# A convolution and sparse-coding kernel: one image buffer instead of two, sums from a ring of 8-row pieces, larger rings, and new orders on every engine

## The chip, the cores and the metric

The kernel runs on one core of a Trainium2 chip. Times are device microseconds of one launch, which works through all 16 images. The core's engines are TensorE (PE), VectorE (DVE), ScalarE (ACT), GpSimd (POOL) and SyncE (SP); each works through its own list of instructions in order, and they wait for each other by semaphores.

## The reference

The input is 16 images of 64 channels, 128 x 128 pixels, in float32. Two layers follow each other, both of the form "x plus something of the group-normalised x":

```
def _gn(v, G=32, eps=1e-5):      # mean and variance over 2 channels x 128 x 128
    g = v.reshape(B_, G, C_ // G, H_, W_)
    return ((g - mean) / sqrt(var + eps)).reshape(v.shape)

x = x + conv3x3_circular(_gn(x), L0_conv_weight)          # 64 -> 64 channels
x = x + patchwise_omp(_gn(x), L1_conv_dictionary)
```

The second layer cuts the image into 4 x 4 patches (1024 per image, each a vector of 64 * 16 = 1024 numbers), and rebuilds each from 5 columns ("atoms") of a dictionary of 512:

```
D = dictionary / (norm(dictionary, axis=0) + 1e-10)
h_bar = D.T @ X                       # correlations
h = h_bar
for k in 1..5:
    index = argmax(|h| where not yet chosen)
    grow a Cholesky factor L by the row of G = D.T @ D + 1e-5 I at the chosen atoms
    x_stack = solve(L L.T, h_bar[chosen]);  h = h_bar - x_stack @ G[chosen]
X_hat = D @ coeffs
```

## The kernel before, in words

An image is held with row pairs: 128 partitions (parity of the row and channel), 64 row pairs, 128 columns. Its work is split over three periods, so that in period `i` the kernel convolves image `i`, does most of the pursuit of image `i-1`, and ends and rebuilds image `i-2`. A period has these parts.

- **Statistics (`st`, ScalarE).** The first normalisation of image `i+1` is a sweep for the sum and one for the squares over each of eight 8-row pieces (L346). The second normalisation sweeps the convolution's result (`junk_sums`). A small product on TensorE (`average`) joins channels, `root` (`rt`) on ScalarE and `gn_part` (`gn`) on VectorE make the factors `fac`, and for the first normalisation the scaled weights `wc`, `wq` and, by the product `bias`, the `shift`.
- **Convolution.** Eight rounds of 12 + 24 matmuls (L1003, L1010, L1012) into one buffer, `conv_ps`. ScalarE moves each round to `xa` (`ev`, L556); only then can the next round start. SyncE loads `xh`, the rows of a round, two rounds ahead.
- **Correlation.** ScalarE makes `z` (L538) for each of 8 tiles of 128 patches, TensorE multiplies it by the atoms (`correlate`, L947), ScalarE moves the result to `h` (`h`, L549).
- **Pursuit.** The tiles are two groups of four. A *unit* is one of the 5 steps of one group of one image. `UNITS` lists the ten units of a period as (how many images back, group, step). In a unit VectorE first finishes the step before it (small algebra, then `project`: L852, L860), then takes four maxima (L743) of scores that ScalarE makes (L605), then finds the indices. GpSimd gathers numbers of the Gram matrix (L466) and its rows (L478) at the chosen atoms.
- **Rebuilding.** `coefficients` (`co`) solves for the five numbers, the plan entry `ce` (VectorE, L648, L638, L654) spreads them over 512 columns for a pair of tiles, TensorE turns each tile (`turn`, L906), ScalarE copies it to `ct` (L517), TensorE multiplies by the atoms (`recon`, L935), ScalarE moves the result to `rb` (`re`, L526), and GpSimd adds a quarter of an image in DRAM (L486).

**What sets the order.** VectorE's and ScalarE's frame is the ten units. A table says what else is done where: place `4 n + s` is unit `n`, and for ScalarE `s` is the score after which it stands (0 to 3). For VectorE `s` is 0 at the unit's start, 1 and 1.5 inside `project`, 2 after the maxima, 2.5 after the aim, 3 after the index search, 3.5 at the end. The tables are `VECTOR_PLAN`, `SCALAR_PLAN`, `ADD_PLAN` (after which unit GpSimd adds), and four of the same kind for the tail, which is what is left when the last convolution is over. TensorE's order is written out in `period` and `tail`. Three PSUM banks are shared by `corr` and `re` in the order of `BANKS`; each waits until ScalarE has moved the one before it in its bank. `room` looks this up.

Buffers around the change: `xa`, two whole images; `ce`, two tiles; `ct`, one group; `rb`, one quarter.

## Time and profile before

| | us |
|---|---|
| time, median of 3 (lowest, highest) | 3507.67 (3506.91, 3508.01) |
| span of the profiled execution | 3506.6 |
| TensorE busy | 3022.3 (86%) |
| VectorE busy | 2678.0 (76%) |
| ScalarE busy | 1724.7 (49%) |
| GpSimd busy | 1858.1 (53%) |

For the profiled execution only its span is given, from the first to the last instruction; it is 1.1 us under the median of the runs. Periods can be told apart by the copy to `shift` (L701), of which there is one per image, shortly before its first convolution. A page's row "busy, mean ns | idle before, releaser" gives the idle time of the engine before such instructions and who ended it. PEclk is the granted clock of TensorE as a share of its full 2.4 GHz.

### The profile page before, as it was taken

Reading aid. Unit: us, or ns where it says so; the run is one execution under the profiler, and the core shown is the slowest. Engines: PE = TensorE matmul, PEld = TensorE weight load, DVE = VectorE, ACT = ScalarE, POOL = GpSimd, SP = SyncE. Lnnn points to the kernel's source line nnn. Section 1 sums busy time; section 2 is a strip of 40 time slices with the busy share of each in tenths; the row PEclk is TensorE's granted clock in tenths of the full one; section 3 lists DMA queues with packets and bytes.
Section 4 is the critical chain, followed back from the end, with each engine's and each line's share of the span. In section 5 each row is a group of like instructions: output and inputs, shape, how many; then the busy total and the mean of one; then the engine's idle time right before and its main releaser. Section 6 shows DMA issues by size and latency. Waiting matters only on the chain.

```text
span 3506.6 us, 33737 instructions
## 1 busy us (share of the span) xinstructions
PE 3022.3 (86%) x9424; PEld 1289.8 (37%) x9424; DVE 2678.0 (76%) x6981; ACT 1724.7 (49%) x2899; POOL 1858.1 (53%) x1869
## 2 busy tenths in 40 slices
PE   4996889899898989989898998989898998985547
PEld 1442333344333333433333333433333443332213
DVE  1137987878788887878789787878878787987982
ACT  3554554645555464655546364554635455443212
POOL 0025555546655564565556555555555565556761
PEclk9998999999999999999999999999999999997778
DMA  3433453435345443534444354445444453441232
GB/s 115 158 130 100 154 136 121 146 94 180 73 156 136 146 134 82 193 75 160 116 146 143 97 168 99 147 104 166 124 127 140 99 159 92 130 108 48 67 66 48
DMA packets 130507, 428.31 MB, mean 122 GB/s; under 512 B 55696, under 2 KB 55952, under 8 KB 105616
## 3 DMA queue, kind: packets, MB, share of 16 engines
q0 software_dynamic: 91776, 204.20, 24.0%
q1 hardware_dynamic: 38544, 221.96, 17.4%
q8 instruction: 76, 1.25, 0.1%
q14 instruction: 111, 0.91, 0.1%
HBM read 289.70 MB, written 136.31 MB: 121 GB/s over the span
## 4 chain that ended last, share of the span: by engine, by line
PE 70%; DVE 15%; issue 7%; POOL 4%; ACT 3%; DMA 1%; ACTq 0%; POOLq 0%; DVEq 0%
PE gen_ps L935 23%; PE gen_ps L947 22%; PE conv_ps L1003 14%; PE conv_ps L1010 7%; POOL v L466 4%; DVE ce L654 3%; DVE u L852 3%; DVE top L743 2%; DVE idx L752 2%; PE ct_ps L906 2%; DVE hot L638 1%; ACT score L605 1%; DVE h L860 1%; PE gen_ps L964 1%; ACT xa L556 1%
## 5 line engine op out<-in xcount | busy, mean ns | idle before, releaser
L466 POOL DMA_INDIRECT v<-gram_rows,cell x1280 | 1262.2, 986 | 1039.3 <-DVE cell L761 669.2
L935 PE MATMUL gen_ps<-ct,dt 128*128 128x512 f32 x2048 | 945.5, 619 | 31.4 <-ACT rb L526 18.5
L947 PE MATMUL gen_ps<-dn,z 128*128 128x512 f32 x2048 | 906.2, 598 | 32.5 <-ACT z L538 31.2
L1003 PE MATMUL conv_ps<-xh,wc 128*128 128x512 f32 x1536 | 707.6, 610 | 48.1 <-ACT xa L556 47.1
L743 DVE MAX8 top<-score 128x8 f32<-128x512 f32 x640 | 420.9, 691 | 424.6 <-ACT score L605 408.6
L478 POOL DMA_INDIRECT u<-marked_rows,chosen x504 | 519.6, 1031 | 187.3 <-issue 153.2
L935 PEld LDWEIGHTS gen_ps<-ct,dt 128*128 128x128 f32 x2048 | 400.1, 199 | 534.5 <-issue 512.9
L947 PEld LDWEIGHTS gen_ps<-dn,z 128*128 128x128 f32 x2048 | 387.7, 192 | 526.2 <-issue 491.6
L605 ACT ACTIVATE score<-h 128x512 f32<-128x512 f32 x640 | 381.8, 604 | 373.6 <-DVE h L860 203.1
L852 DVE SCALAR_TENSOR_TENSOR u<-u,nl 128x512 f32<-128x512 f32 x748 | 512.7, 747 | 12.8 <-DMA u<-marked_rows,chosen 9.3
L526 ACT ACTIVATE rb<-gen_ps 128x512 f32<-128x512 f32 x256 | 277.3, 1101 | 419.6 <-PE gen_ps L935 293.4
L1003 PEld LDWEIGHTS conv_ps<-xh,wc 128*128 128x128 f32 x1536 | 294.2, 195 | 421.1 <-issue 420.0
L752 DVE FIND_INDEX8 idx<-h 128x8 uint32<-128x520 f32 x640 | 432.1, 694 | 0.0
L906 PE MATMUL ct_ps<-ident,ce 128*128 128x128 f32 x512 | 103.9, 338 | 317.1 <-DVE ce L654 272.7
L1012 PE MATMUL conv_ps<-xh,wq 64*64 64x512 f32 x1536 | 359.3, 597 | 0.0
L1010 PE MATMUL conv_ps<-xh,wq 64*64 64x512 f32 x1536 | 359.2, 597 | 0.0
L654 DVE SCALAR_TENSOR_TENSOR ce<-hot,xc,ce 128x512 f32<-128x512 f16 x512 | 359.0, 740 | 0.0
L860 DVE SCALAR_TENSOR_TENSOR h<-u,na,h 128x512 f32<-128x512 f32 x504 | 352.8, 746 | 6.9 <-DMA u<-marked_rows,chosen 5.8
L556 ACT ACTIVATE xa<-conv_ps,shift 128x1024 f32<-128x1024 f32 x128 | 142.5, 1113 | 431.7 <-PE conv_ps L1012 431.7
L538 ACT ACTIVATE z<-xa,fac 128x512 f32<-128x512 f32 x256 | 293.8, 1259 | 97.3 <-PE gen_ps L947 94.2
L906 PEld LDWEIGHTS ct_ps<-ident,ce 128*128 128x128 f32 x512 | 68.9, 168 | 388.1 <-DVE ce L654 291.3
L517 ACT ACTIVATE ct<-ct_ps 128x512 f32<-128x512 f32 x128 | 75.7, 591 | 273.0 <-PE ct_ps L906 220.6
(103 smaller groups left out, 1859.5 us busy)
## 6 DMA issues: line engine op xcount, KB each, us to landing
xh<-x_paired SPq DMA_DIRECT2D x128, 650.0 KB, 4.1
xa<-x_pairs SPq DMA_DIRECT2D x64, 1024.0 KB, 7.2
y_rows<-xa SPq DMA_DIRECT2D x64, 1024.0 KB, 9.3
y_rows<-rb POOLq DMA_DIRECT2D x64, 1024.0 KB, 8.0
v<-gram_rows,cell POOLq DMA_INDIRECT x1280
u<-marked_rows,chosen POOLq DMA_INDIRECT x504, 3.9
dn<-atoms SPq DMA_DIRECT2D x1, 2048.0 KB, 11.5
gram_rows<-u POOLq DMA_DIRECT2D x4, 256.0 KB, 2.4
```

Source lines behind the costliest of these rows:

```text
L466: pool.indirect_dma_start(v[:, g, k - 1, j, t:t + 1], None, cells, bass.IndirectOffsetOnAxis(ap=cell[:, g, k // (KMAX - 1), j, t:t + 1], a ...
L478: pool.indirect_dma_start(kept(img, g, k, t), None, marked, bass.IndirectOffsetOnAxis(ap=chosen[:, g, t:t + 1], axis=0))\
L605: act.activation(score[t % 2][:], h[:, g * T + t, 0:ATOMS], ACT.Abs).then_inc(score_ready[g], 1)
L654: dve.scalar_tensor_tensor(ce[:, place, :], hot[:, m % HOT_RING, :], coef, ce[:, place, :], ALU.mult, ALU.add).then_inc(ce_step, 1)
L743: dve.max(top8[:, t, :], score[t % 2][:]).then_inc(top_found[g], 1)
L752: dve.max_index(idx8[:, t, :], h[:, g * T + t, ATOMS:HW], h[:, g * T + t, :]).then_inc(located[g], 1)
L852: dve.scalar_tensor_tensor(kept(img, g, k, t), kept(img, g, j, t), nl[:, g, k - 1, j, t:t + 1], kept(img, g, k, t), ALU.mult, ALU.add).the ...
L860: dve.scalar_tensor_tensor(hh, kept(img, g, k, t), na[:, g, k, t:t + 1], hh, ALU.mult, ALU.add)\
L935: last = pe.matmul(to[:], dt_[:, a, d, :], ct[:, a, :], start=(a == 0), stop=(a == NA - 1))
L947: last = pe.matmul(to[:], z[:, t % 2, d // PATCH, d % PATCH, :], dn[:, d, :], start=(d == 0), stop=(d == ND - 1))
L1003: pe.matmul(conv_ps[:, a], wc[:, tap, a * CIN:a * CIN + P], rows[:, a + 1:a + 2 * CP:2, tap:tap + W], start=(tap == 0), stop=False)
L1010: pe.matmul(conv_ps[above, a], wq[second, tap, :], rows[second, a:a + 2 * CP - 1:2, tap:tap + W], start=False, stop=(tap == TAPS - 1))
```

## The change

`xa` holds one image instead of two. The image that is only summed for its statistics, the next one, comes in eight pieces of 8 row pairs through a ring `xs` of two, each loaded as soon as the piece two before is summed. So the evictions of the convolution, which write `xa`, wait for the store of the image before and for the `z` that reads it. `ce` has four places instead of two, `ct` two groups instead of one, `rb` two quarters instead of one. All order tables, TensorE's order, the banks and the tail's list of units are new. The lines of the convolution, the correlation, the turns, the reconstruction and the pursuit are as they were.

```diff
+CHUNKS = PAIRS // SWEEP
-CE_RING = 2
+CE_RING = 4
+XS_RING = 2
+RB_RING = 2
+CT_RING = 2
+CHUNK_PLAN = {
+    0: [0, 1, 2], 5: [3, 4], 7: [5, 6, 7],
+}
-TAIL = (... (2, 1, 4), (1, 1, 0), (1, 0, 2), (1, 1, 1), ...
+TAIL = (... (2, 1, 4), (1, 0, 2), (1, 1, 0), (1, 1, 1), ...
 VECTOR_PLAN = {
-    1.5: [("co", 0)], 5: [("ce", 0, 0)], 11: [("ce", 0, 1)], 24: [("co", 1), ("ce", 1, 0)],
-    30: [("ce", 1, 1), ("gn", 1, 1)], 35.5: [("gn", 0, 1)], 38: [("gn", 0, 2)],
+    0: [("co", 0)], 1.5: [("ce", 0, 0)], 9: [("ce", 0, 1)], 23: [("co", 1)], 24: [("ce", 1, 0)], 30: [("ce", 1, 1)],
+    31: [("gn", 1, 1)], 38.5: [("gn", 0, 1), ("gn", 0, 2)],
 }
-ADD_PLAN: 4: [(0, 0)], 6: [(0, 1)], 7: [(1, 0)], 9: [(1, 1)]
+ADD_PLAN: 4: [(0, 0)], 7: [(0, 1)], 9: [(1, 0), (1, 1)]
-        xa = [sb(f"xa{n}", [P, PAIRS, W]) for n in range(2)]
+        xa = sb("xa", [P, PAIRS, W])
+        xs = sb("xs", [P, XS_RING, SWEEP, W])
-        rb = sb("rb", [P, HR, W])
+        rb = sb("rb", [P, RB_RING, HR, W])
-        ct = sb("ct", [P, NA, T * P])
+        ct = sb("ct", [P, CT_RING, NA, T * P])
+        def chunk_in(eng, c, image):
+            eng.dma_start(xs[:, c % XS_RING], x[image][:, c * SWEEP:(c + 1) * SWEEP, :]).then_inc(xs_loaded[c % XS_RING], 16)
 # statistics, first normalisation, images after the first
+                    if not square:
+                        act.wait_ge(xs_loaded[c % XS_RING],
+                                    at(i - 1, 16 * CHUNKS // XS_RING, 16 * (c // XS_RING + 1)))
+                    rows = xs[:, c % XS_RING]
 # SyncE, after round r of the convolution (the loads of whole quarters go)
+                    for c in CHUNK_PLAN.get(r, ()):
+                        if here[-1]:
+                            sp.wait_ge(x_sums[0], at(i + (c >= XS_RING), SUMS[0], 2 * ((c - XS_RING) % CHUNKS) + 3))
+                            chunk_in(sp, c, i + 1)
 # ScalarE, ct
-                    if not (img == 0 and g == 0):
-                        act.wait_ge(recon_done, at(img, GROUPS * ND, g * ND))
+                    if not (img == 0 and g < CT_RING):
+                        act.wait_ge(recon_done, at(img, GROUPS * ND, (g + 1 - CT_RING) * ND))
 # ScalarE, ev
+                    if i > 0 and c % (ROUNDS // GROUPS) == 0:
+                        for ph in range(PHASES):
+                            act.wait_ge(x1_out[c // (ROUNDS // GROUPS) * PHASES + ph], at(i, 16, 0))
+                    if i > 0:
+                        act.wait_ge(z_ready, at(i - 1, TILES, c + 1))
...
```

The order changes, where a period starts on TensorE (here the one of the seventh image). `conv_ps` rows open a round of the convolution, `gen_ps<-dn,z` a correlation, `ct_ps` a turn. Before:

```order
L1003 MATMUL conv_ps<-xh,wc 128x512 [waits rows_loaded0,x1_ready,shift_ready,weights_ready]
...
L1003 MATMUL conv_ps<-xh,wc 128x512 [waits x1_ready,rows_loaded1]
...
L906 MATMUL ct_ps<-ident,ce 128x128 [waits ct_ready,ce_step]
...
L1003 MATMUL conv_ps<-xh,wc 128x512 [waits x1_ready,rows_loaded0]
...
L906 MATMUL ct_ps<-ident,ce 128x128 [waits ct_ready,ce_step]
...
L1003 MATMUL conv_ps<-xh,wc 128x512 [waits x1_ready,rows_loaded1]
...
L947 MATMUL gen_ps0<-dn,z 128x512 [waits recon_out,z_ready]
```

Now:

```order
L1023 MATMUL conv_ps<-xh,wc 128x512 [waits rows_loaded0,x1_ready,shift_ready,weights_ready]
...
L967 MATMUL gen_ps0<-dn,z 128x512 [waits recon_out,z_ready]
...
L1023 MATMUL conv_ps<-xh,wc 128x512 [waits x1_ready,rows_loaded1]
...
L926 MATMUL ct_ps<-ident,ce 128x128 [waits ct_ready,ce_step]
...
L1023 MATMUL conv_ps<-xh,wc 128x512 [waits x1_ready,rows_loaded0]
...
L967 MATMUL gen_ps1<-dn,z 128x512 [waits recon_out,z_ready]
...
L1023 MATMUL conv_ps<-xh,wc 128x512 [waits x1_ready,rows_loaded1]
```

The correlations went from behind round 3 to between the rounds, and the second turn behind round 3.

On VectorE at the start of a period, the rows from the last step of `co` on. Before:

```order
L835 TENSOR_TENSOR xc<-xc,tmp 128x4 [waits solve_step]
L743 MAX top8<-score0 128x8 [waits score_ready1,signed0]
L743 MAX top8<-score1 128x8 [waits score_ready1]
...
L747 TENSOR_TENSOR h<-top8,plus_minus 128x4x8 [waits top_found1]
L752 MAX_INDEX idx8<-h 128x8 [waits aimed1] x4
L755 TENSOR_TENSOR which<-idx8 128x4 [waits located1]
L757 TENSOR_TENSOR chosen<-idx8 128x4
```

Now:

```order
L855 TENSOR_TENSOR xc<-xc,tmp 128x4 [waits solve_step]
L668 TENSOR_SCALAR ce<-count,which,xc 128x512 [waits ce_turned,solve_step]
L668 TENSOR_SCALAR ce<-count,which,xc 128x512 [waits ce_turned]
L658 TENSOR_SCALAR hot<-count,which 128x512 [waits ce_step] x2
L674 SCALAR_TENSOR_TENSOR ce<-hot,xc,ce 128x512 [waits ce_step,hot_step] x2
...
L763 MAX top8<-score0 128x8 [waits score_ready1,signed0]
L763 MAX top8<-score1 128x8 [waits score_ready1]
```

The first `ce` pair stood one unit later and now stands ahead of the period's first maxima.

On ScalarE between the scores of the ninth and the tenth unit, down to the root of the first normalisation (`gsc0`). Before:

```order
L605 ACTIVATE score0<-h 128x512 [waits top_found0,h_updated0]
L605 ACTIVATE score1<-h 128x512 [waits top_found0,h_updated0]
L549 ACTIVATE h<-gen_ps2 128x512 [waits located0,corr_done]
L579 ACTIVATE gsc0<-conv_ps 128x3 [waits gn_sum0]
...
L526 ACTIVATE rb<-gen_ps0 128x512 [waits recon_done]
L526 ACTIVATE rb<-gen_ps1 128x512 [waits recon_done]
L538 ACTIVATE z<-xa1,fac1 128x128x4 [waits corr_done,gn_step1]
L538 ACTIVATE z<-xa1,fac1 128x128x4
L605 ACTIVATE score0<-h 128x512 [waits h_updated1]
```

Now:

```order
L625 ACTIVATE score1<-h 128x512 [waits top_found0,h_updated0]
L350 ACTIVATE xs,sums0<-xs 128x1024 [waits x_sums0,xs_loaded1]
L350 ACTIVATE xs,sums0<-xs,minus_shift0 128x1024 [waits x_sums0]
...
L553 ACTIVATE z<-xa,fac1 128x128x4 [waits corr_done,gn_step1]
...
L564 ACTIVATE h<-gen_ps1 128x512 [waits located0,corr_done]
L564 ACTIVATE h<-gen_ps0 128x512 [waits located0,corr_done]
L625 ACTIVATE score0<-h 128x512 [waits h_updated1]
L625 ACTIVATE score1<-h 128x512 [waits h_updated1]
L599 ACTIVATE gsc0<-conv_ps 128x3 [waits gn_sum0]
```

The last three pieces of the sums and two `h` now stand ahead of the tenth unit's scores, and the root behind the second of these scores.

## Rows read from the trace of the kernel before

**Rows 1.** The page, busy us, share of the span, instructions, for each engine:

```profile
PE 3022.3 (86%) x9424; PEld 1289.8 (37%) x9424; DVE 2678.0 (76%) x6981; ACT 1724.7 (49%) x2899; POOL 1858.1 (53%) x1869
```

**Rows 2.** Windows: one steady period, then three stretches inside it:

```profile
core 0: us, PE busy (x) PEld busy (x) DVE busy (x) ACT busy (x) POOL busy (x), PEclk, DMA share, GB/s
1157.60:1360.00 202.40, 184.79 (x584) 78.71 (x583) 166.00 (x434) 106.91 (x180) 113.66 (x117) 0.96 0.44 131
1241.40:1299.10 57.70, 47.35 (x154) 20.60 (x153) 47.69 (x123) 29.46 (x57) 34.66 (x37) 0.94 0.44 134
1167.00:1175.00 8.00, 7.94 (x36) 3.02 (x36) 8.00 (x16) 1.20 (x2) 4.40 (x4) 1.00 0.97 220
1179.00:1189.00 10.00, 10.00 (x41) 3.82 (x39) 9.80 (x20) 1.80 (x3) 0.00 (x0) 0.83 0.12 48
```

**Rows 3.** TensorE's waits in that period: us in total, times, longest:

```profile
PE ct_ps L906 <- DVE ce L654: 13.2, 2, 9.6
PE conv_ps L1003 <- ACT xa L556: 2.2, 2, 1.4
```

**Rows 4.** VectorE's longest waits in that period:

```profile
DVE top L743 <- ACT score L605: 26.7, 10, 8.4
```

**Rows 5.** TensorE in order of time: start, duration, operation, idle before:

```profile
1157.58 5.33 PE L1003 MATMUL conv_ps<-xh,wc 128*128 128x512 f32 x12
...
1178.76 0.66 PE L906 MATMUL ct_ps<-ident,ce 128*128 128x128 f32 x4 [3.55 <-DVE ce L654]
1179.25 7.02 PE L1003 MATMUL conv_ps<-xh,wc 128*128 128x512 f32 x12
...
1236.25 7.03 PE L947 MATMUL gen_ps<-dn,z 128*128 128x512 f32 x16
1243.12 3.60 PE L935 MATMUL gen_ps<-ct,dt 128*128 128x512 f32 x8
1246.55 5.33 PE L1003 MATMUL conv_ps<-xh,wc 128*128 128x512 f32 x12
...
1254.55 10.57 PE L935 MATMUL gen_ps<-ct,dt 128*128 128x512 f32 x24
```

**Rows 6.** VectorE in order of time, maxima of the first unit and first `ce` pair:

```profile
1158.96 2.73 DVE L743 MAX8 top<-score 128x8 f32<-128x512 f32 x4 [3.75 <-ACT score L605]
...
1170.88 1.01 DVE L648 TENSOR_SCALAR ce<-count,which,xc 128x512 f32<-128x512 f16 x2
...
1177.96 1.40 DVE L654 SCALAR_TENSOR_TENSOR ce<-hot,xc,ce 128x512 f32<-128x512 f16 x2
```

**Rows 7.** ScalarE's groups in that period: busy us, mean ns, idle before:

```profile
L538 ACT ACTIVATE z<-xa,fac 128x512 f32<-128x512 f32 x16 | 18.4, 1260 | 5.9 <-PE gen_ps L947 5.9
...
L346 ACT ACTIVATE xa<-xa,minus_shift 128x1024 f32<-128x1024 f32 x8 | 9.2, 1147 | 0.2
```

**Rows 8.** VectorE in order of time: copies to `shift` of images 1, 2, 3, 15:

```profile
171.88 0.16 DVE L701 COPY shift<-conv_ps 128x1 f32<-128x1 f32 x1 [10.42 <-PE conv_ps L989]
...
337.13 0.14 DVE L701 COPY shift<-conv_ps 128x1 f32<-128x1 f32 x1
...
540.80 0.14 DVE L701 COPY shift<-conv_ps 128x1 f32<-128x1 f32 x1
...
2968.07 0.14 DVE L701 COPY shift<-conv_ps 128x1 f32<-128x1 f32 x1
```

**Rows 9.** The page's DMA issues: KB each, median us from issue to landing:

```profile
xh<-x_paired SPq DMA_DIRECT2D x128, 650.0 KB, 4.1
xa<-x_pairs SPq DMA_DIRECT2D x64, 1024.0 KB, 7.2
```

**Rows 10.** Waits behind the last period (3181.4 to 3507), then order of time:

```profile
DVE ce L648 <- PE ct_ps L906: 9.4, 2, 5.0
...
ACT rb L526 <- DMA y_rows<-rb: 42.2, 5, 17.0
...
3452.87 0.63 PE L906 MATMUL ct_ps<-ident,ce 128*128 128x128 f32 x4 [0.84 <-ACT ct L517]
...
3460.07 1.41 DVE L654 SCALAR_TENSOR_TENSOR ce<-hot,xc,ce 128x512 f32<-128x512 f16 x2
```

More of the change, by code:

```diff
@@ L162, in lag @@
         return 0 if n < T else 1
[L163 removed]
+    return 2 if kind in ("co", "ce", "ct", "re") else 0
 def units(i, images):
@@ L455, in _ @@
                 sp.wait_ge(x1_out[n], 16 * images)
-            sp.wait_ge(recon_added, 16 * GROUPS * PHASES * images)
+            for n in range(RB_RING):
+                sp.wait_ge(recon_added[n], 16 * GROUPS * PHASES * images // RB_RING)
         @block.gpsimd
@@ L472, in gather @@
                     if img == images - 1 and g == 1 and k == 2:
-                        for n in range(GROUPS * PHASES):
-                            pool.wait_ge(x1_out[n], at(img, 16, 0))
-                        pool.wait_ge(z_ready, at(img, TILES, 0))
+                        pool.wait_ge(x_sums[0], at(img, SUMS[0], SUMS[0]))
+                    elif img == images - 1 and g == 1 and k == 3:
+                        pool.wait_ge(conv_done, at(img, ROUNDS, ROUNDS))
                     for t in range(T):
@@ L536, in extra @@
                         first = (t // T * PHASES + ph) * HR + t % T * CP
-                        rows = xa[q][:, first:first + CP, :]
+                        rows = xa[:, first:first + CP, :]
                         last = act.activation(z[:, t % 2, ph].rearrange("p j (h w) -> p h w j", h=TP // 2),
@@ L934, in recon @@
                 for a in range(NA):
-                    last = pe.matmul(to[:], dt_[:, a, d, :], ct[:, a, :], start=(a == 0), stop=(a == NA - 1))
+                    last = pe.matmul(to[:], dt_[:, a, d, :], ct[:, g % CT_RING, a, :], start=(a == 0), stop=(a == NA - 1))
                 last.then_inc(recon_done, 1)
@@ L1021, in convolve, with period @@
                     turn_atoms(c)
-            def period(i, par):
+            def period(i):
                 here = parts(i)
@@ L1027, in period @@
                     convolve(i, 0)
+                if b:
+                    correlate(i, 1, 4)
+                if own:
                     convolve(i, 1)
@@ L1043, in period @@
                     correlate(i, 1, 6)
+                if own:
+                    convolve(i, 5)
+                if b:
+                    correlate(i, 1, 7)
                 if p:
@@ L1062, in period @@
                 if p:
-                    turn(i - 2, 1, 0)
                     recon(i, 2, 0, 4)
@@ L1066, in period @@
                     recon(i, 2, 0, 6)
+                    turn(i - 2, 1, 1)
                     recon(i, 2, 0, 7)
@@ L1070, in period @@
                 if p:
-                    turn(i - 2, 1, 1)
                     turn(i - 2, 1, 2)
@@ L1085, in period @@
                     correlate(i, 0, 1)
+                if here[-1]:
+                    average(i + 1, 0)
+                if own:
                     correlate(i, 0, 2)
                 if here[-1]:
-                    bias(i + 1, 1 - par)
+                    bias(i + 1, (i + 1) % 2)
                 if p:
@@ L1107, in tail @@
                 recon(i, 2, 0, 2)
+                turn(i - 2, 1, 0)
+                turn(i - 2, 1, 1)
                 recon(i, 2, 0, 3)
@@ L1119, in tail @@
                 recon(i, 2, 1, 2)
+                turn(i - 1, 0, 0)
                 recon(i, 2, 1, 3)
@@ L1152, in _ @@
             for i in range(images):
-                period(i, i % 2)
+                period(i)
             tail(images)
```

146 lines of the change are left out of this document (71 added, 75 removed), and 70 rows, old and new, of tables (BANKS, SCALAR_PLAN, TAIL_BANKS, TAIL_SCALAR_PLAN).

## The prediction, made before the changed kernel ran

> **What bounds the kernel now.** I read the page first: TensorE is busy 86% of the span, VectorE 76%, ScalarE 49% [rows 1]. A share over the span hides where it waits, so next came one steady period in a windows query: of 202.40 us TensorE is busy 184.79, VectorE 166.00, ScalarE 106.91 [rows 2]. So TensorE stands still for 17.6 us in a period, and the list of waits says for what: 13.2 us at L906, for a `ce` that VectorE has not built (two times, the longest 9.6), and 2.2 us for the eviction L556 of the convolution buffer [rows 3]. VectorE has 36.4 us free per period, yet 26.7 us of it is spent waiting for a score that ScalarE gives late [rows 4]. The two engines wait for each other at different places of the period: no resource is full, the order is what costs.
>
> The waits cost twice. After the 3.55 us stop, the 12 matmuls of L1003 take 7.02 us, where the same 12 take 5.33 undisturbed [rows 5]; the granted clock of that stretch is 0.83 (part of it at 1.2 GHz instead of 2.4), after a stop of 1.4 us it stays at 1.00 [rows 2]. After the 9.6 us stop it is slow again; by the same ratio of 1.3 I put the two together at 4 to 5 us per period. TensorE's floor for a period is then 184.8 - 4.8 = 180. It is also the sum of its parts from undisturbed starts: a convolution 8.00, a correlation 6.87, a reconstruction 3.43 [rows 5], 8 x 8.0 + 8 x 6.95 + 16 x 3.47 + 8 turns of 0.47 + 0.5 = 179.5.
>
> **The new period, by hand.** Time 0 is the start of convolution 0. I lay the new orders along three engines with the durations of today; no instruction that computes is removed or added in a steady period but for one tiny sum.
>
> *VectorE, start.* Today the four maxima of the first unit wait 3.75 us and end at 1161.7, which is 4.1 after convolution 0 (1157.58) [rows 5, 6]; the first `ce` pair stands a unit later and takes 8.4 us (1170.88 to 1179.36 [rows 6]). The change puts the pair before these maxima, where the wait was. They need the last correlation of the period before, so they still end near 4.1 and the 8.4 us go out of what follows. The turn that waited 3.55 us finds its `ce` ready.
> *TensorE, start.* Convolution 0 ends at 8.0; correlation 4 now stands between it and convolution 1 and covers the eviction (the 1.4 us wait goes): 15, 23. Convolution 2 waits 0.8 for its eviction: 32. Correlation 5: 39. Convolution 3 needs eviction 2, which stands behind the scores of the third unit, ready near 39.3, so it starts at 41 (a new wait of 1.5) and ends at 49; convolution 4 ends at 58, correlation 6 at 65, convolution 5 at 73, correlation 7 at 80.
> *Meeting point 1.* The sixth unit's last score needs correlation 7. VectorE is there early: from the first maxima to the sixth unit's it takes 79.7 us today, of which 8.4 are the moved pair and about 3 are waits, so 68.3; it arrives at 73 and is let go at about 82.
> *VectorE to the last `ce` pair.* Today 57.7 us, 47.7 of them busy [rows 2]; with the maxima taken off it is 46.4 of work, and I find under 1 us of waiting left, since the scores between stand behind work that TensorE finished earlier. The last pair is ready at 129.
> *TensorE to the same point.* Two turns, two convolutions, eight reconstructions and one more turn from 80: 127. So the stop of 9.6 us becomes one of 1.7 to 2.
> *Second half.* Two turns, eight reconstructions, four correlations, the two small products: 58 us from 129, so convolution 0 of the next image starts at 187. On the way the bias product (which cannot go before VectorE's `fac`) is reached at 169.4. VectorE's factor steps moved from between units 9 and 10 to behind the last maxima; these wait for scores that stand behind 12 us of ScalarE (three chunks at two sweeps of up to 1.15 [rows 7] and their read-outs, 2.4 each, the closing sums 1.3, one z of two times 1.26 [rows 7], two h of 0.6) and I get 168.3 for `fac`. It is hidden by 1.1 us only. VectorE then has `co` and the first `ce` pair done at 187.8 and closes the loop at its 4.1.
> Sum of the waits left: 0.8 + 1.5 + 0.7 + 2 + 3 x 0.7 = 7.1 over 179.5 to 180, which is the 187 again. With half a microsecond for handovers that I didn't count, 187.5 against 202.27 (2968.07 - 540.80 over 12 periods [rows 8]). All remaining stops but one are shorter than the 1.4 us that left the clock alone today, so I charge no slow clock.
>
> **The other edits.** *One image buffer, eight chunks.* Bytes are the same; a chunk is half of the old piece. Cost on ScalarE: the same 16 sweeps, a `few` of one column instead of four. A chunk's load can be late: 650 KB land in 4.1 us, 1 MB in 7.2 [rows 9], so 512 KB take between 2 and 7.2, and by the line through both rows 3.0. Seven chunks are asked for 10 us or more ahead; the eighth is asked for when chunk 5 is summed and wanted 4.8 us later, so it is hidden at 3.0 and costs 7.2 - 4.8 - 1.1 = 1.3 per period at the upper end. *SyncE's order.* Row piece 3 now stands behind chunk 2, which waits for the first chunk's sums at 27; landed at 31, wanted at 41. *New waits of the evictions* (for the store of the old image and for z): the stores are issued half a period before, the z it needs is always ahead of it on ScalarE. Nothing, upper end 1 us. *Two `rb`, two `ct`, four `ce`.* ScalarE's waits for the added store are off TensorE's path in a steady period; the 42.2 us of them behind the last period [rows 10] count at the end. GpSimd keeps its order of gathers; the first add stands before the sixth unit's four rows and waits to 106, the rows land by 113 and are wanted from 114: hidden by about 1 us.
>
> The Trainium skill speaks against the chunks: "DMA: Bandwidth & Descriptors", section "Rules for kernel authors", wants many small transfers joined into one, and the section on the anatomy of one DMA puts the fixed part near 2 us, an estimate of 8 us per image if nothing hid it. The landing times in the rows already hold that part, and the sum goes by them.
>
> **Start and end.** The period of image 0 is a full TensorE without anything to wait for: 0. Image 1: today 165.3 from shift to shift [rows 8], with ScalarE's evictions holding the scores back; the new order has one less, I take 4 less (0 to 8). Image 2: 203.7 today; VectorE comes late into it, as it does today, and now the first correlation stands before it, so I take 8 less instead of 15 (0 to 15). Behind the last period: VectorE waited 9.4 us for a free `ce` place and ScalarE 42.2 for `rb` [rows 10]; both go. What is late next is TensorE's own reconstructions before the last turns, free at 3453.5 against 3461.5 for the last `ce` today: 8 gained there, 4 more from the moved first pair: 12 (4 to 20), since the gathers that the last coefficients wait for stay.
>
> **Sum.** 13 periods x 14.8 = 192; 12 for images 1 and 2; 12 at the end: 216. The profiled execution has a span of 3506.6, which gives 3290.6; the median of the runs is 1.1 above the span, so 3292.
>
> **Rivals.**
> 1. *ScalarE's long lists decide* (chance 0.22). Seventeen entries stand between the scores of the eighth and ninth unit, twelve microseconds of them between the ninth's and tenth's. ScalarE does them in order, each with a wait of its own. Beyond the 1.1 us of cover every microsecond of lateness there goes through the bias product into TensorE. For: 36.4 us of VectorE's idle are now almost all of this kind [rows 4]. Against: ScalarE is only half busy. With 4 to 10 us of it per period the period is 191.5 to 198 and the time 3345 to 3430.
> 2. *No wait is left at the `ce`* (0.17). If evictions come without lag and VectorE loses its remaining waits, the period goes to 182 to 184: 3215 to 3250.
> 3. *Short stops slow the clock* (0.04). Ten stops of 0.7 to 2 us remain. If each slows one convolution by 1.69 (7.02 - 5.33 [rows 5]), the period gains 10 and the gain shrinks to about 60: 3420 to 3450. The row of today speaks against it: clock 1.00 behind the 1.4 us stop [rows 2]. The skill's "TensorE: Matmul & The Clock Gate", section "A second HAM failure mode: psum-queue depth-cycling", describes such loss from frequent small stops; today's trace doesn't show it.
> 4. *Slower than before* (0.07). The evictions of convolutions 1, 2 and 7 stand later among VectorE's units (behind units 2, 3 and 8), so TensorE's single convolution buffer is held by VectorE's pace. If VectorE enters the period not at 4.1 but 20 us late, as image 2 shows for a fill period, convolutions 1 to 3 wait, correlation 7 comes 15 to 20 us late, and the sixth unit with it: the loop closes at more than VectorE's 166 + 36. It decides from 15 us of lateness per period; price 3 to 8 us per period, 3550 to 3610. Against: VectorE's load of 166 leaves 21 us in a period of 187 to catch up.
> 5. *It cancels out* (0.03): between these, within 0.2% of the time of before (7 us, about what can be told from no change).
>
> **Numbers.** Forecast 0.47 with 3250 to 3340. Faster by over 0.2%: 0.90; within: 0.03; slower: 0.07. To hold 8 in 10, the range takes in most of rivals 1 and 2: 3220 to 3400.
>
> **What would show it.** The shift copies 187 to 188 us apart. TensorE's wait at the turns for `ce` falling from 13.2 to about 2 per period, with a new one of 1 to 2 before convolution 3 for the eviction. PEclk near 1.00 in steady slices. VectorE's longest wait at the sixth unit's last maximum (about 6 us), not at the tenth unit. The bias product without a wait. It is wrong if TensorE waits at the bias product or for z (rival 1), if the chunk sums wait for a load, or if SyncE is late with the image rows.

## The result and the profile after

The changed kernel takes 3401.2 us (median of 4 runs, 3394.1 to 3408.0) beside 3507.3 for the kernel before: a ratio of 0.970, 95% interval 0.9685 to 0.9714. That is 106 us faster, where 216 were predicted; 3401.2 lies 1.2 us above the upper end of the range. The profiled execution took 3408.0 us, with a span of 3406.1. All times here are medians of undisturbed executions: one execution of the run f4, of 8684 us, and one slow execution each of h2 and j2 are left out.

The page of the changed kernel; the first row answers to [rows 1], the last two are its chain of waits:

```profile
PE 3012.6 (88%) x9424; PEld 1276.3 (37%) x9424; DVE 2681.5 (79%) x6981; ACT 1717.0 (50%) x2899; POOL 1989.0 (58%) x1869
...
PEclk9997999999999999999999999999999999997778
...
PE 33%; POOL 23%; DVE 17%; issue 11%; DMA 10%; ACT 4%; ACTq 0%; POOLq 0%; DVEq 0%
```

TensorE's and VectorE's busy times are as before, within 10 us. GpSimd's busy time rose from 1858 to 1989 us though it issues the same 1869 instructions, and it now makes 23% of the chain that ended last. This is the row to stop at: the same gathers have become longer.

VectorE in order of time, copies to `shift` of images 1, 2, 3 and 15, as in [rows 8]:

```profile
170.76 0.16 DVE L721 COPY shift<-conv_ps 128x1 f32<-128x1 f32 x1 [3.55 <-PE conv_ps L1009]
...
333.27 0.16 DVE L721 COPY shift<-conv_ps 128x1 f32<-128x1 f32 x1 [2.89 <-PE conv_ps L1009]
...
531.86 0.16 DVE L721 COPY shift<-conv_ps 128x1 f32<-128x1 f32 x1 [0.90 <-PE conv_ps L1009]
...
2882.65 0.16 DVE L721 COPY shift<-conv_ps 128x1 f32<-128x1 f32 x1 [0.59 <-PE conv_ps L1009]
```

The steady period is (2882.65 - 531.86) / 12 = 195.90 us, against 202.27 before and 187.5 predicted. Image 1 takes 162.5 (165.3 before), image 2 198.6 (203.7), and from the last copy to the end of the span, which takes in the thirteenth period too, it is 523.5 (538.5).

Windows query of the changed kernel, one steady period from convolution 0 to the next, then the convolution behind the stop that is shown below and one behind a short stop; the columns are those of [rows 2]:

```profile
1327.53:1522.80 195.27, 184.02 (x584) 77.92 (x583) 165.96 (x435) 106.52 (x180) 125.17 (x119) 0.98 0.46 136
...
1394.91:1402.10 7.19, 7.19 (x16) 2.89 (x20) 6.70 (x18) 4.43 (x8) 4.85 (x5) 0.76 0.02 4
1376.52:1382.00 5.48, 5.48 (x16) 2.30 (x20) 4.79 (x8) 3.65 (x8) 4.26 (x5) 1.00 0.99 371
```

TensorE's waits in that period, then VectorE's, which answer to [rows 3, 4]:

```profile
PE conv_ps L1023 <- ACT xa L576: 4.8, 3, 3.2
PE gen_ps L955 <- ACT rb L541: 3.4, 1, 3.4
...
PE ct_ps L926 <- DVE ce L674: 0.9, 1, 0.9
...
DVE top L763 <- ACT score L625: 9.1, 5, 5.0
DVE tmp L794 <- DMA v<-gram_rows,cell: 4.8, 1, 4.8
DVE u L872 <- DMA u<-marked_rows,chosen: 4.7, 4, 2.2
DVE h L880 <- DMA u<-marked_rows,chosen: 2.6, 2, 2.3
```

The wait for `ce` fell from 13.2 us to 0.9, and VectorE's wait for scores from 26.7 to 9.1. In their place VectorE waits 13.7 us for what GpSimd gathers (12.1 for rows and Gram numbers as shown, 1.6 for the last Gram numbers; 4.4 in the period of before), and TensorE 3.2 us for the eviction of convolution 4. The two belong together. Here is GpSimd in order of time while VectorE builds the second `ce` pair (start, duration, operation, idle before):

```profile
1351.50 0.94 POOL L476 DMA_INDIRECT v<-gram_rows,cell  x1 [10.52 <-DVE cell L781]
1352.74 0.96 POOL L476 DMA_INDIRECT v<-gram_rows,cell  x1 [0.31 <-issue]
1354.01 1.02 POOL L476 DMA_INDIRECT v<-gram_rows,cell  x1 [0.30 <-issue]
1355.33 1.29 POOL L476 DMA_INDIRECT v<-gram_rows,cell  x1 [0.30 <-issue]
1356.92 6.57 POOL L476 DMA_INDIRECT v<-gram_rows,cell  x1 [0.30 <-issue]
```

and VectorE over the same time, then where it misses that gather:

```profile
1353.87 0.60 DVE L658 TENSOR_SCALAR hot<-count,which 128x512 f16<-128x512 f16 x2
1354.39 1.41 DVE L674 SCALAR_TENSOR_TENSOR ce<-hot,xc,ce 128x512 f32<-128x512 f16 x2
...
1359.94 1.41 DVE L674 SCALAR_TENSOR_TENSOR ce<-hot,xc,ce 128x512 f32<-128x512 f16 x2
1361.26 1.41 DVE L880 SCALAR_TENSOR_TENSOR h<-u,na,h 128x512 f32<-128x512 f32 x2
...
1373.68 0.17 DVE L794 TENSOR_TENSOR tmp<-nl,v 128x8 f32<-128x8 f32 x1 [4.78 <-DMA v<-gram_rows,cell]
```

A gather takes 0.94 us and the next begins 1.25 us after it. The one at 1356.92 takes 6.57 us: it ends at 1363.49, 0.8 us after VectorE has finished the pair and the two `h` updates behind it (1362.67). Where no `h` update follows, it is 5.25 us and ends 0.8 us after the pair. I call a single gather of more than 2.5 us *held*. The changed kernel has 29 of them, 169 us in all; the kernel before has 4. In the changed kernel all 29 lie inside the building of a `ce` pair, among the 323 gathers that begin there; none of the 1469 gathers elsewhere is held. The last row is the cost: the third unit's algebra waits 4.78 us for its numbers. That delay goes on to the scores, and to the eviction that stands behind them on ScalarE, and so to TensorE:

```profile
1390.38 1.20 ACT L625 ACTIVATE score<-h 128x512 f32<-128x512 f32 x2 [7.61 <-DVE top L763]
1391.51 2.29 ACT L553 ACTIVATE z<-xa,fac 128x512 f32<-128x512 f32 x2
1393.60 1.07 ACT L576 ACTIVATE xa<-conv_ps,shift 128x1024 f32<-128x1024 f32 x1
```

```profile
1394.91 5.37 PE L1023 MATMUL conv_ps<-xh,wc 128*128 128x512 f32 x8 [3.18 <-ACT xa L576]
```

The first fence is ScalarE, the second TensorE at the start of convolution 5. Behind this stop the granted clock is 0.76, in part at 1.2 GHz instead of 2.4, and the convolution's first part takes 7.19 us instead of 5.48 (the last two rows of the windows above). So the stop costs nearly 5 us.

### The profile page after: what moved, and what is told of

Same layout as the page of the kernel before. It is cut to its first block, busy times and chain, and to the rows that moved or that the text cites. A ratio compares the mean times of both kernels' runs of the same rounds, so it can differ in the third digit from the quotient of the medians.

```text
span 3406.1 us, 33931 instructions
## 1 busy us (share of the span) xinstructions
PE 3012.6 (88%) x9424; PEld 1276.3 (37%) x9424; DVE 2681.5 (79%) x6981; ACT 1717.0 (50%) x2899; POOL 1989.0 (58%) x1869
## 3 DMA queue, kind: packets, MB, share of 16 engines
q8 instruction: 76, 1.25, 0.1%
## 4 chain that ended last, share of the span: by engine, by line
PE 33%; POOL 23%; DVE 17%; issue 11%; DMA 10%; ACT 4%; ACTq 0%; POOLq 0%; DVEq 0%
POOL v L476 20%; PE gen_ps L967 14%; PE gen_ps L955 10%; DMA u<-marked_rows,chosen 9%; DVE u L872 5%; PE conv_ps L1023 4%; DVE idx L772 4%; DVE top L763 3%; POOL u L489 2%; PE conv_ps L1030 2%; DVE h L880 2%; ACT score L625 1%; DVE ce L674 1%; ACT z L553 1%; PE gen_ps L984 1%
## 5 line engine op out<-in xcount | busy, mean ns | idle before, releaser
L476 POOL DMA_INDIRECT v<-gram_rows,cell x1280 | 1386.3, 1083 | 861.2 <-DVE cell L781 496.8
L880 DVE SCALAR_TENSOR_TENSOR h<-u,na,h 128x512 f32<-128x512 f32 x504 | 355.7, 747 | 49.2 <-DMA u<-marked_rows,chosen 48.5
L674 DVE SCALAR_TENSOR_TENSOR ce<-hot,xc,ce 128x512 f32<-128x512 f16 x512 | 359.3, 741 | 0.0
L926 PE MATMUL ct_ps<-ident,ce 128*128 128x128 f32 x512 | 85.8, 293 | 143.2 <-DVE ce L674 74.6
L1030 PEld LDWEIGHTS conv_ps<-xh,wq 64*64 64x64 f32 x1536 | 102.0, 131 | 238.4 <-issue 238.4
```

The source lines that it names most:

```text
L476: pool.indirect_dma_start(v[:, g, k - 1, j, t:t + 1], None, cells, bass.IndirectOffsetOnAxis(ap=cell[:, g, k // (KMAX - 1), j, t:t + 1], a ...
L674: dve.scalar_tensor_tensor(ce[:, place, :], hot[:, m % HOT_RING, :], coef, ce[:, place, :], ALU.mult, ALU.add).then_inc(ce_step, 1)
L880: dve.scalar_tensor_tensor(hh, kept(img, g, k, t), na[:, g, k, t:t + 1], hh, ALU.mult, ALU.add)\
L1030: pe.matmul(conv_ps[above, a], wq[second, tap, :], rows[second, a:a + 2 * CP - 1:2, tap:tap + W], start=False, stop=(tap == TAPS - 1))
```

## The experiments

Three theories were set against each other. R: the held gathers wait for room for descriptors. B: transfers (adds, chunk loads, image rows) fill the DMA engines and rows land late. P: VectorE's building of a `ce` pair holds GpSimd off, at certain phases of the two. S is the prediction's first rival, ScalarE's long lists. (M, in some of the expectations, is the theory that the fast form of L658 has no part in it.)

One thing has to be said on the numbers. The runs went to different chips. On two of them (e and i) the kernel before takes 3505 to 3506 us, on the others (f, h, j) 3888 to 3890, and there TensorE is stopped at places where the first chips show nothing. Times are compared only with runs of the same kind. Each group of runs went to another chip at another time, so an effect of the chip can't be told from one of the hour.

**Room for descriptors, and adds apart.**

```
e1: dynamic_dma_scratch_size=8192  ->  4096
e4: ADD_PLAN 9: [(1, 0), (1, 1)]   ->  8: [(1, 0)], 9: [(1, 1)]
```

> One edit to the changed kernel (3401 us): the memory for GpSimd's DMA descriptors is halved, from 8192 to 4096. All orders, loads and stores are as they were. Theory R (room for descriptors: a gather that reaches fixed places in the count of GpSimd's DMAs waits until earlier ones have landed): the places come twice as often, so single gathers of more than 2.5 us rise from 29 to 50 or more, VectorE's waits for gathered rows (u and h behind marked_rows, 128 us together in the whole run) grow, and the time is 3415 to 3480. Theory B (bandwidth: rows only land late because loads and adds occupy the DMA engines): nothing of this changes, 3401 within 8. Rival S (ScalarE's long lists set the loss): also 3401 within 8.

> One edit to the changed kernel (3401 us): the adds (1,0) and (1,1), issued back to back behind unit 9's rows, are issued one behind unit 8's rows and one behind unit 9's. Theory B (adds back to back fill the DMA engines for some 19 us at a period's start, and the rows for the second and third unit land late): VectorE's 4.8 us wait in the third unit falls, the period goes from 195.9 down by 2 to 4, 3350 to 3375. Theory R (places in the count of descriptors): the count at which the adds come shifts for only a few gathers, so the long gathers stay at about two per period and the time stays within 10 of 3401, unless the new wait of the add (1,0) for its last eviction delays the rows behind it, then up to 3420.

e1: 3408.9 us (ratio 0.9731, 0.9715 to 0.9747), 21 held gathers. e4: 3410.4 us (0.9722, 0.9705 to 0.9738), 29 held gathers, period 197.1. R expected 50 or more held gathers in e1; halving the room gave fewer. B expected e4 to gain 26 us or more; it is 9 slower. The 6.57 us gather of each period stands at the same place in all of them.

**One `rb`.** e6 is e4 with `RB_RING = 1`; e7 is e6 with 16384 bytes for descriptors.

> Two edits to the changed kernel (3401 us): the adds stand one by one (as in the run before this) and there is one rb instead of two. It is the control for the next run, since one rb sets 8 KB free. ScalarE's first eviction of a reconstruction then waits until the add before it has landed, 7 to 15 us at a time. In a steady period that is off TensorE's path by my prediction (0 to 15 us per run), at the end it costs up to 42 us less what TensorE does meanwhile: 3410 to 3470. If the second rb carries much of the gain, it is over 3470 and TensorE waits for rb in the steady periods.

> As the run before this (one rb, adds one by one), and the 8 KB that this sets free go to GpSimd's descriptors: 16384 instead of 8192. Theory R: the long gathers (5.25 or 6.57 us, about two per period) vanish or halve, VectorE's waits for gathered rows fall by 40 us or more in the whole run, and it is 30 to 80 us faster than the run before this. Theory B: the same time within 8 us of the run before this, with the rows landing just as late. Rival S: the same time too.

e6: 3902.2 us (1.114, 1.110 to 1.118), e7: 3896.7 (1.112, 1.109 to 1.115), with 28 and 23 held gathers: twice the room changes nothing, and R is out. The surprise is e6 itself, 492 us slower than e4. Its waits, whole run:

```profile
ACT rb L541 <- DMA y_rows<-rb: 589.8, 35, 29.1
...
PE gen_ps L955 <- ACT rb L541: 433.5, 43, 17.0
```

ScalarE stands up to 29 us for an added store, and TensorE behind it: 33 us per period (230.1 against e4's 197.1). I read it so: the new orders put the adds late among the gathers and lean on the second buffer. I had costed it at nothing in a steady period.

**The fast form, and the phase.**

```
f1, h1, i1 (L658, write and read in steps of two):
- dve.tensor_scalar(hot[:, m % HOT_RING, :], count[:], ...)
+ dve.tensor_scalar(hot[:, m % HOT_RING, :].rearrange("p (a b) -> p b a", b=2),
+                   count[:].rearrange("p (a b) -> p b a", b=2), ...)
f2, h2, i2 (ahead of the second pair of group 0):
+ if (g, pair) == (0, 1):
+     dve.tensor_reduce(idle[:], count[:], axis=AX.X, op=ALU.add)
f4, j3: the kernel before, an idle sum over 700 elements of `dn` ahead of every pair
g1, h3, i3: the new buffers under the old tables and TensorE's old code,
            CHUNK_PLAN = {0: [0, 1], 4: [2], 5: [3], 6: [4], 7: [5, 6, 7]}
```

> One edit to the changed kernel (3401 us): the one-hot rows `hot` (L658) are written and read in steps of two elements, so that VectorE takes them at its plain speed, some 0.5 us instead of 0.27 each, 32 of them per image: 8 us more work for VectorE in a period of 195.9. Theory P (the long gathers come from VectorE: all 29 single gathers over 2.5 us of the changed kernel lie inside the building of a `ce` pair, none of the 1469 outside; the fast form of L658 keeps GpSimd from writing a gather's descriptors until the pair is built): no gather over 2.5 us is left, VectorE's waits for gathered rows and products fall, and the time is within 3350 to 3440, since VectorE's added work costs about what it gives back. Theory M (it is the two-input instructions L674 that hold GpSimd off, or the DMA traffic): the long gathers stay at 20 to 30, and the time is 3440 to 3500.

> One edit to the changed kernel (3401 us): one idle VectorE instruction of about 0.55 us (a sum over `count`, its result unused) stands ahead of the second `ce` pair of a period, which begins in step with a gather. Theory P: in the stretches that are hit, GpSimd's gathers start 0.13 and 1.46 us after L658 begins and the third, at 3.05, is held to the end; where they start 0.4 us before it, none is. With the pair 0.55 us later the 6.57 us gather of each period vanishes (16 of the 29 go), and the period falls by 2 to 5 us: 3335 to 3375. Theory B or S (contention of transfers, ScalarE): VectorE has 0.55 us more to do per period, 3401 to 3412, with the rows as late as before.

> One edit to the kernel before (3507 us): an idle VectorE instruction of about 0.75 us ahead of every `ce` pair, four per image. Theory P: it moves the pairs from the harmless phase (gathers 0.4 us ahead of L638) into the harmful one (about 0.13 behind, with a gather pitch of 1.25 us), so single gathers over 2.5 us rise from 4 to 30 or more. Its work alone is 3 us per period of VectorE, which has 36 us free; with the held gathers it is 3525 to 3600. Without the theory: 4 to 8 long gathers as today, 3507 to 3530.

> The changed kernel's buffers (one image buffer with 8-row chunks, four `ce`, two `ct`, two `rb`) under the orders of the kernel before: its tables for VectorE, ScalarE and GpSimd's adds, its unit order at the end, its PSUM banks, and TensorE's code as it was. Only the chunk loads are spread over SyncE's rounds 0 to 7 so that nothing waits in a circle. By my prediction the steady gain comes from the orders: the two waits for `ce` (13.2 us per period) stay, the period stays at 200 to 203, and only the end is shorter (up to 20 us): 3475 to 3510. If the buffers carry the gain (the run with one rb was 500 us slower than the changed kernel), it is 3400 to 3450, and the period is near 196.

These four fell on a chip where the kernel before takes 3887.5 us: f1 3923.3 (1.010, 1.008 to 1.012), f2 3970.1 (1.022, 1.020 to 1.025), f4 4084.9 (1.050, 1.0475 to 1.0524), g1 3968.3 (1.021, 1.019 to 1.023). Held gathers inside pairs: 2, 12, 12 and 21 (g1 has three shorter ones, up to 4.5 us, outside). P had expected 30 or more for f4. Against each other they could be read, against 3401 not, so the changed kernel went beside them.

> The changed kernel itself, unedited, as a control beside the next three: the chip of the last four runs took 3888 us for the kernel before, not 3505, so those four can't be compared with 3401. If this chip is like the first, 3395 to 3408, with the kernel before at 3505; on a chip like the last one I expect the changed kernel at 3880 to 3960, for f1 and f2 were slower than the kernel before there.

> As f1: the one-hot rows at VectorE's plain speed, beside the changed kernel on the same chip. Theory P: at most 2 single gathers over 2.5 us (29 in the changed kernel), VectorE's waits for gathered rows and products down by 40 us or more over the run, against 8 us per period of added work: within 40 us of the control, either side. Theory M (the fast form has no part in it): 20 or more long gathers, and 40 to 100 us slower than the control.

> As f2: an idle instruction of 0.55 us ahead of the second `ce` pair. f2 showed no long gather in the second pair any more, 12 in the first. Theory P: 10 to 14 long gathers instead of 29, none in the second pair, and 25 to 60 us faster than the control (5.3 us less lateness of the third unit's products and rows per period, of which VectorE and TensorE feel 2 to 4). If TensorE does not feel these gathers (rival S, ScalarE's lists set the loss), the time is the control's within 8 us though the long gathers are gone.

> As g1: the changed kernel's buffers under the orders of the kernel before, now beside the changed kernel on the same chip. By my prediction the buffers alone bring 0 to 20 us and the orders the rest: 3475 to 3510 where the kernel before takes 3505, period 200 to 203. If the buffers carry the gain, it is within 30 us of the control.

The kernel before took 3889.7 us again, so this was such a chip too. h0: 3962.0 (1.019, 1.014 to 1.024), h1: 3916.3 (1.009, 1.006 to 1.012), h2: 3970.8 (1.018, 1.013 to 1.023), h3: 3967.2 (1.021, 1.019 to 1.023). Held gathers inside pairs: 20, 2, 7, 21 (h3 has five more outside, up to 4.2 us). On such a chip the changed kernel is 2% slower than the kernel before. h1 is 46 us faster than h0. h2 is 9 us slower, inside the scatter, though it has 13 held gathers fewer: on this chip that is nearer to what S expected (within 8 us) than to P's 25 to 60 us faster. The last section shows what else stops TensorE there.

> As f1 and h1 (one-hot rows at VectorE's plain speed), on another chip. On the slow chips it was 46 us faster than the changed kernel with 2 long gathers instead of some 20. If the kernel before takes 3505 here: theory P 3350 to 3410 with at most 4 long gathers; theory M or S 3430 to 3500, because VectorE has 8 us more to do per period. If the kernel before takes 3888 here, 3910 to 3930 as on the last chip.

> As f2 and h2 (0.55 us of idle VectorE work ahead of the second `ce` pair), on another chip. If the kernel before takes 3505 here: theory P 3340 to 3380, about 13 long gathers, all in the first pair of a period; theory S or B 3395 to 3412 although the second pair's long gathers are gone. If the kernel before takes 3888, 3940 to 4000 as on the last chip.

> As g1 and h3 (new buffers, old orders), on another chip. On the slow chips it took the changed kernel's time. If the kernel before takes 3505 here: by my prediction 3475 to 3510, the orders carrying the gain; if the buffers carry it, 3400 to 3430. If the kernel before takes 3888, 3960 to 3975.

Here the kernel before took 3506.3 us, so these stand beside 3401.2; the changed kernel itself was not run on this chip, but its ratio of 0.970 (0.9685 to 0.9714) can be set against the ratios here. i1: 3373.0 (0.962, 0.9605 to 0.9637), 6 held gathers where at most 4 were expected. **i2: 3350.4 (0.955, 0.9533 to 0.9565), 22 held gathers.** i3: 3596.1 (1.025, 1.024 to 1.027), 10 held gathers inside pairs and 7 outside, up to 3.1 us.

i2 decides between the theories: one VectorE instruction more (0.67 us, its result unused) makes the kernel 51 us faster, and it beats both kernels. GpSimd during the same pair in i2, whose L658 begins at 1330.2:

```profile
1328.62 0.95 POOL L477 DMA_INDIRECT v<-gram_rows,cell  x1 [0.30 <-issue]
1329.87 0.94 POOL L477 DMA_INDIRECT v<-gram_rows,cell  x1 [0.30 <-issue]
1331.12 1.28 POOL L477 DMA_INDIRECT v<-gram_rows,cell  x1 [0.30 <-issue]
1332.71 0.95 POOL L477 DMA_INDIRECT v<-gram_rows,cell  x1 [0.30 <-issue]
1333.96 0.95 POOL L477 DMA_INDIRECT v<-gram_rows,cell  x1 [0.31 <-issue]
```

The gathers now begin 0.4 us ahead of L658 instead of 0.14 behind it, and none is held. Held gathers in this second pair fell from 13 to 3 over the run (in the third they rose from 5 to 10, which explains why there are 22 and not the 13 that were expected). The steady period is (2824.50 - 521.55) / 12 = 191.9 us:

```profile
521.55 0.16 DVE L724 COPY shift<-conv_ps 128x1 f32<-128x1 f32 x1 [0.59 <-PE conv_ps L1012]
...
2824.50 0.16 DVE L724 COPY shift<-conv_ps 128x1 f32<-128x1 f32 x1 [0.56 <-PE conv_ps L1012]
```

and in the period from 1286.31 the waits of TensorE and VectorE are these:

```profile
PE gen_ps L958 <- ACT rb L542: 3.4, 1, 3.4
PE ct_ps L929 <- DVE ce L677: 2.4, 1, 2.4
PE conv_ps L1026 <- ACT xa L577: 1.7, 2, 0.8
...
DVE top L766 <- ACT score L626: 12.4, 7, 5.0
DVE h L883 <- DMA u<-marked_rows,chosen: 2.7, 2, 2.4
DVE u L875 <- DMA u<-marked_rows,chosen: 2.6, 1, 2.6
```

The 4.8 us wait for `v` is gone, and with it TensorE's 3.2 us at convolution 5, which starts 64.0 us after convolution 0 (median over 11 periods) instead of 67.8. Theory B would have left both, and S would have left the time.

Each of the two traces holds one period that shows the same without an edit. In the changed kernel's period from 1135.1 the gathers happen to begin 0.38 us ahead of L658 and none is held in the second pair: convolution 5 starts at 64.0 and the period is 192.4 us, where the ten others are 194.5 to 198.0. In i2's period from 1686.1 a gather in the second pair is held for 8.15 us: convolution 5 starts at 69.4 and the period is 199.5 us, where the ten others are 189.9 to 192.0; VectorE's 4.8 us wait for `v` and a 4.9 us wait of TensorE for an eviction are back. (Two more gathers are held later in that period, which adds to its length but not to the start of convolution 5.) So it is the held gather that delays convolution 5, and not something else that the idle instruction moves.

i1 agrees: it gives VectorE more work (each pair takes 8.6 us from its first L658 on instead of 7.5, so 4 us per period; I had expected 8) and is 28 us faster. It doesn't say which of the two instructions holds GpSimd off. A held gather (5.92 us) still occurs, and L658 takes 0.50 us there instead of 0.34; whether a fast form is left in it no run shows. One thing the traces do show: the 6.57 us gathers stay held through two `h` updates (L880), which are not of L658's form, so a hold that has begun lasts as long as this chain of VectorE.

i3 refutes what was expected of it, both ways: neither 3475 to 3510 nor near the changed kernel. ScalarE waits for chunks 31 times there:

```profile
ACT xs L351 <- DMA xs<-x_pairs: 294.1, 31, 12.6
```

My reading is that the old order of the sums wants a chunk soon after its slot came free. So buffers and orders can't be told apart by taking one of them: the new buffers without their orders lose 90 us against the kernel before, the new orders without the second `rb` lose 492 against e4.

**What was left.**

> i2 (0.55 us of idle VectorE work ahead of the second `ce` pair) with one more edit: in the first pair of each group-0 row the one-hot rows are made at VectorE's plain speed, 2 us more work per period. In i2 22 long gathers are left, few of them in the pairs that this touches (4 in the first pair). Theory P: 2 to 5 fewer of them, -10 to +15 us against i2 (3350), since the added work and the gathers freed about cancel; it is the version to beat i2, if one does.

> i2 with one more edit: the add (0,0) stands behind the rows of the sixth unit (one place later) instead of ahead of them. In the changed kernel GpSimd waits there 9 us for ScalarE's fourth eviction of a reconstruction, and the sixth unit's rows land that much later. Theory A (the early add is a part of what is left): VectorE's waits for u and h rows at the seventh unit go, period 191.9 down by 1 to 3, 3315 to 3340. Rival (the second rb then comes free too late for ScalarE, as with one rb): 3360 to 3420.

> As f4, now at the speed of the first chip: the kernel before with about 0.75 us of idle VectorE work ahead of each `ce` pair. Theory P: long gathers rise from 4 to 12 or more and the time from 3505 to 3520 or more, up to 3570, beyond the 3 us per period of work that VectorE's 36 us of free time should hide. If the kernel before is proof against it (its pairs lie where TensorE's waits leave room), 3505 to 3520.

```
j1: i2, with the steps of two in the pair (0, 0) alone
j2: i2, with ADD_PLAN 4: [(0, 0)]  ->  5: [(0, 0)]
```

The kernel before took 3888.1 us, so these answer only in part. j1: 3965.8 (1.019, 1.015 to 1.023), as h2, with 10 held gathers (j2 has 18). j2: 3917.6 (1.005, 1.002 to 1.009), 48 us faster than j1 beside it and 53 faster than h2 on a chip of the same kind: on these chips the early add does cost. j3: 4087.0 (1.052, 1.048 to 1.055) with 14 held gathers, 199 us for 3.5 us of added work per period (four idle sums of 0.87); whether the held gathers make that can't be said, as no trace of the unedited kernel on such a chip exists. How j1 and j2 do at the speed of the first chips is not known.

## Why the prediction was wrong

The period of 187.5 us failed; most of the steps around it held. 8.4 us per period (195.9 - 187.5) over 13 periods are 109 us, and the time is 109 us above the forecast of 3292. (That the two agree so closely is partly luck: the period is read from the profiled execution, which is 6.8 us longer than the median.)

- *TensorE, start.* Predicted: convolutions 1, 2 and 3 at 15, 24 and 41. Measured: 15.0, 24.5 and 39.5; the new wait of 1.5 us for eviction 2 did not come. Right within 1.5 us. Convolution 5 was predicted at 65; it starts at 67.8, and at 64.0 in i2.
- *The step that failed: "Meeting point 1" and "VectorE to the last `ce` pair", 68.3 us of work and then "under 1 us of waiting left", the last pair at 129.* Measured: 137.4 (median of 11 periods), 8.4 late, as much as the period is too long. I took the durations of today for every instruction and looked only at the order of the waits. The gathers' durations and landings did not stay: the second pair now starts in step with a gather, the gather is held for 6.57 us, and VectorE waits 13.7 us for GpSimd's data in a period, where "under 1 us" was reckoned. With the phase moved (i2) the last pair is ready at 132.3, and 51 of the 109 us come back. The other 58 i2 doesn't test: 22 gathers are still held in it.
- *GpSimd's first add "waits to 106, the rows land by 113 and are wanted from 114: hidden by about 1 us".* Wrong by 7 us. The add is issued at 1440.87, 113.3 after convolution 0, and VectorE waits 2.6 us in that period for the rows behind it:

```profile
1440.87 0.99 POOL L497 DMA_DIRECT2D y_rows<-rb  x1 [9.12 <-ACT rb L541]
1442.17 1.03 POOL L489 DMA_INDIRECT u<-marked_rows,chosen  x1 [0.30 <-issue]
```

  j2 supports it as a cause on the slower chips; on the others it is argued from the 2.7 us that VectorE still waits for `h` rows in i2. This, the other held gathers and the eviction of `rb` are what I see of the 4.4 us that i2 keeps above 187.5; that they are all of it, and how much each is, isn't shown.
- *VectorE's longest wait at the sixth unit's last maximum, about 6 us.* In the changed kernel it is 2.2 us, since VectorE comes late; in i2 it is 5.0, as predicted.
- *Turn wait of 1.7 to 2.* 0.9 in the changed kernel, 2.4 in i2. Ahead of these turns TensorE has a wait of 3.4 us that I did not have, for ScalarE's eviction into `rb`; while the `ce` comes later still, it costs nothing.
- *Second half 58 us.* 58.5. *Bias product hidden by 1.1 us:* it doesn't wait in a steady period. *Eighth chunk hidden:* VectorE and TensorE never wait for it; ScalarE waits 11.4 us for chunks in the whole run, and a chunk lands in 3.8 us where 3.0 was reckoned. *No slow clock:* right for the short stops (1.00 behind convolution 4's), wrong for the 3.2 us stop, which wasn't foreseen (0.76). Over the whole period the granted clock is 0.98 (0.96 before).
- *Image 1, image 2, end.* Predicted 4, 8 and, behind the last of the 13 periods, 12 less. Measured 2.7 and 5.1; the last period ends at 3097.3 with this correlation, 308.8 us ahead of the end of the span, where it was 325.2 (3506.6 - 3181.4 [rows 10]), so 16.4 less. Sum 24.2 against 24: the errors cancel, which is luck.

```profile
3090.30 7.03 PE L967 MATMUL gen_ps<-dn,z 128*128 128x512 f32 x16
```

- *Rival 1, ScalarE's lists.* Its range, 3345 to 3430, held the time, but not its mechanism: VectorE's wait for scores fell to 9.1 us, and TensorE waits neither at the bias product nor for z in the steady period.
- *Rival 4, slower than before.* The first chips say no. On the one slower chip where it ran (h0) the changed kernel is slower, while convolutions 1 to 3 start there within 1.6 us of where they do on the first chips, so not by the rival's mechanism.

The Trainium skill has the rule that I should have weighed: "SBUF — State Buffer", section "SBUF: two separate sides", says that descriptors of a DMA issued by GpSimd are written by GpSimd, and that VectorE's fast forms lock it out of the port that it needs for that, for the whole instruction. By that rule I would have looked at each `ce` pair against the gathers. The runs agree that VectorE is what holds them (i2), but not in the size: one L658 takes 0.34 us, a held gather 5.25 or 6.57, and 294 of the 323 gathers inside pairs are not held at all.

## What to carry to other kernels

When a change moves a block of one engine's work beside another engine's stream, the durations of that stream can change: look in the trace of before for its rare long instances (here 4 of 1792 gathers) and at what ran beside them, and put a price on their becoming regular. In the profile after, compare each engine's busy time at an equal count of instructions first; a rise on an engine that was taken to be off the path (here GpSimd, +131 us) can be the first sign. Longer rings and the order that uses them can be one change, and a test that takes only one of them away measures a third kernel.

## What the runs showed of the hardware

- **Held gathers depend on phase.** L658 and L674 repeat with a pitch of 1.85 us, gathers with 1.25. In the changed kernel's trace 62 pairs have three gathers or more beside them. In 29 a gather begins 3.03 to 3.06 us after the pair's first L658, and each of these is held, for 5.25 us, or 6.57. In the other 33 the gather of that time begins at 2.39 to 2.46 us, and none is held. Half a microsecond of phase decides. The other traces from chips where the kernel before takes 3505 to 3508 us, with an unedited L658 (before, e1, e4, e6, e7, i2, i3), say the same: 127 of 127 gathers that begin near 3.05 us are held, and none of 267 that begin at 2.3 to 2.5. On the slower chips most are (18 of 20 in h0). The few other held gathers inside pairs begin at 1.03 to 1.47 us. Why these phases and no others is not known.
- **Some chips run this kernel 11 to 16% slower.** On them the records show TensorE's matmuls ended, and ScalarE and SyncE, which both wait for that convolution, let go 12 us later at the same moment. The changed kernel there (h0), TensorE, ScalarE and SyncE behind convolution 3:

```profile
1328.30 0.66 PE L926 MATMUL ct_ps<-ident,ce 128*128 128x128 f32 x4
...
1342.07 1.19 PE L1023 MATMUL conv_ps<-xh,wc 128*128 128x512 f32 x1 [13.11 <-issue]
```

```profile
1340.71 1.11 ACT L576 ACTIVATE xa<-conv_ps,shift 128x1024 f32<-128x1024 f32 x1 [20.15 <-remote]
```

```profile
1307.21 33.83 SPq L333 DMA_DIRECT2D xh<-x_paired  x3
```

  (the last ends at 1341.04, with the third of its loads). ScalarE's eviction comes 12 us after the convolution's last matmul. Behind convolution 5 it comes 25 us after it (1367.4 to 1392.2), and meanwhile, 33 us after the first release, four transposes of TensorE are up to 2 us apart where they take 0.66 us together elsewhere:

```profile
1374.62 0.27 PE L926 MATMUL ct_ps<-ident,ce 128*128 128x128 f32 x1
1376.72 0.27 PE L926 MATMUL ct_ps<-ident,ce 128*128 128x128 f32 x1 [1.83 <-issue]
1377.41 0.34 PE L926 MATMUL ct_ps<-ident,ce 128*128 128x128 f32 x1 [0.43 <-issue]
1379.51 0.37 PE L926 MATMUL ct_ps<-ident,ce 128*128 128x128 f32 x1 [1.76 <-issue]
```

  TensorE has other work during part of both delays: it loses 13.1 us to the first and 17.6 to the second (13.6 before convolution 6, 4.0 between the transposes). That is 31 us of the 37 that the period of 233.1 us has above 195.9. The cause is open: no run was made for it, and the profile names only "remote" and "issue".
